# An MoE, attention, MoE kernel on one core: the first expert loop waits per expert for its split weights, and eleven of the sixteen low halves are split inside its tiles

## The reference

```python
def ffn(x, W_gate, b_gate, W_e, b_e):          # 8 experts of 512 x 512
    logits = x @ W_gate + b_gate
    _, top_idx = jax.lax.top_k(logits, 2)
    y_all = relu(einsum('bsd,edh->bseh', x, W_e) + b_e)
    return take_along_axis(y_all, top_idx[..., None], axis=2).mean(axis=2)

x = x + 0.5 * ffn(layernorm(x))
x = x + attention(layernorm(x))                # one head of width 128
x = x + 0.5 * ffn(layernorm(x))
```

## Time and profile before

| | us |
|---|---|
| runs | 308.06, 308.17, 309.02 |
| median | 308.17 |
| the profiled execution, own time | 310.12 |
| its span, first to last instruction | 308.4 |

### The profile page before, as it was taken

One profiled execution on the slowest core, in us unless ns is written; L12 is line 12 of the kernel. 1 busy time (PEld: TensorE's weight loads), 2 busy tenths in 40 slices (PEclk: granted clock), 3 DMA queues, 4 the chain that ended last, 5 costly groups with the idle time before them and its releaser, 6 DMA issues. The chain is left out here.

```text
span 308.4 us, 4811 instructions
## 1 busy us (share of the span) xinstructions
PE 250.2 (81%) x1271; PEld 183.7 (60%) x1272; DVE 182.6 (59%) x387; ACT 98.5 (32%) x177; POOL 148.7 (48%) x152
## 2 busy tenths in 40 slices
PE   6828717799999999976999996639999999999500
PEld 2404403488888888844878774314888888888300
DVE  3999999534444443477778657783344344443691
ACT  0654805123323324211324534211223323324100
POOL 4482682636566565324954500005366566563450
PEclk9575755999999999997999998956999999999955
DMA  7996820584444434624130111103354434345892
GB/s 251 382 403 206 315 83 0 145 272 161 145 162 143 131 130 160 198 68 141 67 136 2 68 70 57 56 26 102 104 167 156 150 129 152 123 159 201 268 344 94
DMA packets 22434, 47.24 MB, mean 153 GB/s; under 512 B 4237, under 2 KB 4877, under 8 KB 22417
## 3 DMA queue, kind: packets, MB, share of 16 engines
q0 software_dynamic: 7360, 20.46, 20.6%
q1 hardware_dynamic: 12208, 22.35, 20.5%
q10 hardware_dynamic: 2850, 4.23, 3.7%
HBM read 32.34 MB, written 18.35 MB: 164 GB/s over the span
## 5 line engine op out<-in xcount | busy, mean ns | idle before, releaser
L447 POOL DMA_INDIRECT z_dram<-yrow,place x46 | 46.8, 1017 | 59.8 <-ACT yrow L574 50.3
L1100 DVE TENSOR_TENSOR xt_lo<-tp_ps,xt_hi 128x512 fp32r<-128x512 f32 x46 | 31.8, 692 | 57.6 <-ACT xt_hi L567 56.4
L439 POOL DMA_INDIRECT xg<-xn_dram,tok x46 | 46.4, 1009 | 33.7 <-DVE tok L1087 18.7
L574 ACT ACTIVATE yrow<-ypre 128x512 f32<-128x512 f32 x46 | 29.1, 632 | 100.7 <-DVE ypre L1108 62.1
L567 ACT ACTIVATE xt_hi<-tp_ps 128x512 fp32r<-128x512 f32 x46 | 26.8, 582 | 11.8 <-PE tp_ps L748 11.8
L748 PE MATMUL tp_ps<-ident,xg 128*128 128x128 f32 x184 | 28.2, 277 | 2.0 <-DMA xg<-xn_dram,tok 1.6
L432 POOL TENSOR_TENSOR rstd<-var_eps,neg_half 128x2 f32<-128x2 f32 x12 | 9.4, 786 | 42.1 <-DVE var_eps L953 39.9
L1108 DVE TENSOR_TENSOR ypre<-y_ps,be_bc 128x512 f32<-128x512 f32 x24 | 16.6, 692 | 21.8 <-PE y_ps L763 21.8
L748 PEld LDWEIGHTS tp_ps<-ident,xg 128*128 128x128 f32 x184 | 22.9, 141 | 10.1 <-DMA xg<-xn_dram,tok 2.6
L763 PE MATMUL y_ps<-whi,xt_hi 128*128 x96 | 28.1, 415 | 0.7 <-issue 0.7
L763 PE MATMUL y_ps<-whi,xt_lo 128*128 x96 | 26.3, 396 | 0.0
(11 more groups left out here) (138 smaller groups left out, 395.7 us busy)
## 6 DMA issues: line engine op xcount, KB each, us to landing
raw<-in_L_ffn_W_e_dram SPq DMA_DIRECT2D x16, 512.0 KB, 6.3
z_rows<-z_dram SPq DMA_DIRECT2D x8, 512.0 KB, 3.8
xn_dram<-xn ACTq DMA_DIRECT2D x12, 256.0 KB, 2.2
x<-in_L_attn_x_dram SPq DMA_DIRECT2D x4, 512.0 KB, 5.7
z_last<-z_dram SPq DMA_DIRECT2D x4, 512.0 KB, 5.9
out_dram<-x SPq DMA_DIRECT2D x8, 256.0 KB, 3.7
xn_dram<-xn_more ACTq DMA_DIRECT2D x4, 256.0 KB, 2.7
z_rows<-z_dram SPq DMA_DIRECT2D x4, 256.0 KB, 2.8
```

Of the source, the lines that this page charges most:

```text
L439: pool.indirect_dma_start(out=xg[:, t % XG, :], out_offset=None, in_=xn_dram[f][:, :], in_offset=bass.IndirectOffsetOnAxis(ap=tok[:, t:t + ...
L447: pool.indirect_dma_start(out=z_dram[f][:, :], out_offset=bass.IndirectOffsetOnAxis(ap=place[:, t:t + 1], axis=0), in_=yrow[:, t % YB, :], ...
L574: act.activation(yrow[:, t % YB, :], ypre[:, t % 2, :], ACT.Relu, scale=HALF_MEAN).then_inc(yrow_made, 1)
L1100: dve.tensor_tensor(xt_lo[:, t % 2, :], tp_ps[(n0 + t) % 2][:], xt_hi[:, t % 2, :].bitcast(F32), ALU.subtract).then_inc(xt_made, 1)
```

## The change

It touches the program up to the end of tile 7 of the first expert loop.

- **Waits.** TensorE no longer waits for all weights ahead of the loop. Product t (t < 8) of the first loop waits until 2(t + 1) high and as many low halves are made. The list gives each expert at least one tile (`thresh` is -1 for the first count), so tile t never belongs to an expert above t. The first eight tiles are therefore written out (`HEADS`), and two rounds of six and three single tiles follow.
- **Splits.** GpSimd makes no low halves. VectorE makes 0 and 1 between the batches, 2 to 4 after the list, and 5 to 15 inside tiles 0 to 6 (2, 2, 2, 2, 1, 1, 1), between `lo_rows(t + 1)` and `bias(t)`. ScalarE makes high halves 0 to 10 ahead of the loop (one per batch from the second batch on, the rest around the mark) and 11 to 15 in tiles 0 to 4, behind `relu(t)`.
- **x and its norm.** x is loaded by tiles. ScalarE normalises, as Identity with scale rstd and bias `off` = -mean * rstd; VectorE computes `off` per batch, one batch behind its moments.
- **Biases.** Two loads on SP's queue broadcast them to all partitions (4 experts each, half of `be_bc`). VectorE waits for the first at tile 0 and for the second at tile 4. The matmuls and copies for them are gone.
- **SP's queue.** x by tiles, halves 0 to 7, the eight stores of xn (until now on ScalarE's queue, each waits for its tile), the first bias load, halves 8 to 15, the second bias load. `raw` has room for all, so `AHEAD` is gone.
- **Warm-ups.** 12 instead of 6 at the start, 3 ahead of the first gate, 2 after each gate, 4 and 12 around the last count; 10 instead of 14 after the list; the 6 ahead of the loop are gone.

```diff
-        WARM = [14, 10]
-        WARM_SPLIT = 6
+        WARM = [10, 10]
...
-        DVE_HALVES = [1, 3, 5, 7, 12, 13, 14, 15]
-        POOL_HALVES = [n for n in range(2 * E) if n not in DVE_HALVES]
-        BE_ACT = [E - 2, E - 1]
+        HI_AHEAD = 11
+        LO_AHEAD = 5
+        LO_IN_TILE = [2, 2, 2, 2, 1, 1, 1]
...
-        HEAD, STEP = 2, 6
+        HEADS, STEP = (E, 2), 6
...
@@ sync
+            for i in range(NT):
+                sp.dma_start(x[:, i, :], x_rows[i * P:(i + 1) * P, :]).then_inc(x_in_sem[i], 16)
+            for n in range(E):
+                load_half(n)
+            for i in range(NT):
+                sp.wait_ge(xn_made, i + 1)
+                sp.dma_start(xn_dram[0][i * P:(i + 1) * P, :], xn_at(i)).then_inc(xn_stored[i], 16)
+            load_be(0)
+            for n in range(E, 2 * E):
+                load_half(n)
+            load_be(1)
...
@@ gpsimd
-            for n in POOL_HALVES:
-                split_lo(pool, n, lo_made_pool)
...
@@ scalar
+            def normalise(i):
+                act.wait_ge(off_made, i // TB + 1)
+                act.activation(xn_at(i), x[:, i, :], ACT.Identity, bias=off[:, i:i + 1],
+                               scale=rstd[:, i:i + 1]).then_inc(xn_made, 1)
...
+                hi_left = list(range(HI_AHEAD, 2 * E)) if f == 0 else []
                 hi_rows(0, n0 + 1, None)
-                for t in range(HEAD + STEP):
+                for t in range(head + first * STEP):
                     tile(t)
+                    if hi_left:
+                        split_hi(hi_left.pop(0))
...
@@ tensor
+                    if f == 0 and t < E:
+                        pe.wait_ge(hi_made, 2 * (t + 1))
+                        pe.wait_ge(lo_made, 2 * (t + 1))
...
-                if f == 0:
-                    warm_up(WARM_SPLIT)
-
-                    pe.wait_ge(lo_made_dve, len(DVE_HALVES))
-                    pe.wait_ge(lo_made_pool, len(POOL_HALVES))
-                    pe.wait_ge(be_copied, E - len(BE_ACT))
-                    pe.wait_ge(be_copied_act, len(BE_ACT))
...
                 gate(0, b)
+                warm_up(2, sp_ps)
...
+            warm_up(4, sp_ps)
             count(0, B - 1)
-            broadcast_be(biases.pop(0))
+            warm_up(12, sp_ps)
             token_list(0)
...
@@ vector
                 def tile(t):
                     if t + 1 < NS:
                         lo_rows(t + 1, n0 + t + 2)
+                    if f == 0 and t < len(LO_IN_TILE):
+                        for _ in range(LO_IN_TILE[t]):
+                            split_lo(dve, halves.pop(0), lo_made)
                     bias(t, t, f * NS + t + 1, f * NS + t - 1 if f or t >= 2 else None)
```

More of the change, by code:

```diff
@@ L324, in _, with load_half @@
         def _(sp):
[L325 to L331, removed]
+            def load_half(n):
                 rows = w_e[n // 2].rearrange("(c p) h -> p c h", p=P)
@@ L612, in softmax @@
                                    accum_out=psumrow[:, q:q + 1]).then_inc(prob_made, 1)
+            his = list(range(HI_AHEAD))
+            for i in range(TB):
+                normalise(i)
             act.wait_ge(gate_in, 32)
             for b in range(B):
+                for i in range(TB * (b + 1), min(TB * (b + 2), NT)):
+                    normalise(i)
                 if b:
@@ L618, in _ @@
                 copy_gate(0, b)
[L619 to L620 removed]
+                if b:
+                    split_hi(his.pop(0))
             copy_logits(0, B - 1)
[L622 removed]
+            while len(his) > 3:
+                split_hi(his.pop(0))
+            mark_partition(0)
+            for n in his:
                 split_hi(n)
[L624 to L630 removed]
             experts(0)
@@ L797, in experts @@
                                 r * STEP + (f * NS + t - 1))
-                for t in range(REST, NS):
+                for t in range(REST[f], NS):
                     tile(t)
@@ L858, in _ @@
             pe.wait_ge(const_made, PE_CONSTS)
-            warm_up(6)
-            pe.wait_ge(be_in, 16)
-            biases = list(range(E))
-            for _ in range(2):
-                broadcast_be(biases.pop(0))
+            warm_up(12)
             for b in range(B):
@@ L1089, in route @@
                     tile_experts(f)
-                for n in halves_left:
-                    split_lo(dve, n, lo_made_dve)
-                count_sent(f)
+                if f:
+                    count_sent(f)
             def experts(f):
@@ L1109, in bias @@
                                       be_bc[:, bass.ds(e * H, H)], ALU.add).then_inc(ypre_made, 1)
+                halves = list(range(LO_AHEAD, 2 * E)) if f == 0 else []
                 def tile(t):
@@ L1158, in add_bv @@
                                   ).then_inc(v_made, 1)
-            biases = [e for e in range(E) if e not in BE_ACT]
             for b in range(B):
-                dve.wait_ge(x_in_sem[b], 16)
                 moments("g0", b)
                 if b:
-                    normalise("g0", b - 1)
-            normalise("g0", B - 1)
-            for _ in range(2):
-                copy_be(biases.pop(0))
+                    offsets(b - 1)
+            offsets(B - 1)
             dve.wait_ge(const_made, CONSTS)
-            todo = list(DVE_HALVES)
-            split_lo(dve, todo.pop(0), lo_made_dve)
-            for b in range(B):
-                copy_be(biases.pop(0))
-                if b:
-                    split_rank(0, b - 1)
-                choose(0, b)
-                if b + 1 < B:
-                    split_lo(dve, todo.pop(0), lo_made_dve)
-                if b:
-                    row_hots(0, b - 1)
-            route(0, todo)
+            choose(0, 0)
+            split_lo(dve, 0, lo_made)
+            choose(0, 1)
+            split_rank(0, 0)
+            row_hots(0, 0)
+            split_lo(dve, 1, lo_made)
+            choose(0, 2)
+            split_rank(0, 1)
+            row_hots(0, 1)
+            choose(0, 3)
+            split_rank(0, 2)
+            row_hots(0, 2)
+            route(0)
+            for n in range(2, LO_AHEAD):
+                split_lo(dve, n, lo_made)
             experts(0)
```

113 lines of the change are left out of this document (53 added, 60 removed).

## The result

| | before | after |
|---|---|---|
| runs | 308.06 to 309.25, 4 | 304.61 to 306.40, 4 |
| median, us | 308.60 | 304.94 |
| the profiled execution, own time | 310.12 | 304.77 |
| its span | 308.4 | 303.0 |

The ratio of after to before is 0.9881 [0.9851, 0.9912]: faster by 1.2%. I had forecast 304.0 (298 to 309). The profiled execution of before lay 1.5 us above its median and that of after did not, so the two traces differ by more (5.4 us) than the medians (3.7). A run over 1.5% above the fastest of its kernel counts as slow and is left out; that was so for one run of all, in `best5`.

The account below looks back on a forecast made before the run. The prediction took VectorE, slowed by GpSimd's splits, to bound the lead-in, with gathers holding product 0. A gain of 15.4 us there less 11.2 lost in the loop gave -4.2: 304.0 us against the median, range 298 to 309.

Parts of the forecast that it names:

- What bounds the kernel: Lead-in before product 0: VectorE bounds it, ten instructions losing 11.9 us beside GpSimd; gathers, not the weight wait, hold product 0.
- The list: End of the lead-in: token list ready at 35.5 us (33.8 to 39.9), against 52.01 before.
- a round of ScalarE: Lead-in, per batch: two normalisations, logits, two gate copies and a split on ScalarE take 4.0 us.
- my slower round: Lead-in, per batch: TensorE at the lower clock takes 5.0 us, putting the last gate copy at 27.6.
- From the list to product 0: First gathers and transposes: 7.9 us with three splits beside them, plus 1.1 for traffic; product 0 at 44.5.
- The traffic term: First gathers: loads on SP's queue until about 40 us delay them by 1.1 us (0 to 4.2).
- The ring: First loop's early tiles: VectorE and ScalarE steps wait on each other in a circle, 5.75 us a tile against 3.24; 10.7 lost.
- 0.5 for the clock: First loop: 0.5 us added because TensorE, idle some 2 us in each slowed tile, may lose clock.
- The sum: Whole kernel: 15.4 us gained in the lead-in, 11.2 lost in the loop, -4.2; 304.0 against the median.
- A: First loop: splits hide behind VectorE's and ScalarE's room, only four tiles losing 0.5 us each; 294.8, chance 0.08.
- B: First loop, tiles 3 to 6: TensorE at the lower clock, 6.5 us a tile, 15.1 lost; 307.9 to 311.2, chance 0.14.
- C: First gathers: transfers delay them 4.2 us, product 0 at 47.6; 307.1, or 309 and more with late weights; chance 0.12.

Follow-up runs that it names:

- best5: Changed kernel with bias(t) ahead of the lo splits, nine lo halves ahead of the loop, 30 warm-ups behind the list, late loads spread over several tiles: 295.88 us, 0.9554.
- wait_only: The kernel before with only the waits per expert and the eight tiles written out, all else as it was: 308.67 us, 0.9996 of before.
- gpsimd_beside: The changed kernel plus six 128x1024 subtractions on GpSimd that feed nothing, in the lead-in: 307.94 us, 0.9962 of before.
- loads_late: The changed kernel with raw halves 11 to 15 and the second bias load issued behind the third gather's landing: 300.54 us, 0.9745 of before.
- no_warm: The changed kernel without TensorE's warm-ups between the batches and around the last count: 304.49 us, 0.9856 of before.
- bias_first: The changed kernel with bias(t) moved ahead of the lo splits of tile t on VectorE: 297.20 us, 0.9620 of before.

## Why the prediction was right

- **What bounds the kernel.** Right: the wait for all weights held nothing (`wait_only`), GpSimd stretched VectorE (`gpsimd_beside`, 5.9 us on five instructions; for ten, my rows gave 11.9), and the gathers stood before product 0.
- **The list, 31.2 against 35.5 (33.8 to 39.9).** The one number outside its bounds, on the good side. The first gate copies ended at 11.6 (12.6). My terms for a round of ScalarE add up to 4.0 us, but I summed three rounds of 3.8. In these I had also counted a normalising pair and a split too many: two pairs were left (the third batch's and the fourth's), and the last split stands behind the last copy, where I counted it again. The three rounds took 9.7 together, though a normalisation cost 0.81 on ScalarE, not 0.63, and the last copy ended at 21.3 instead of 24. From there to the list 9.9 us passed, against 9.8 by my working without the warm-ups' delay. The 1.7 us that I had added for that delay and TensorE's lower clock did not come: PEclk was 1.00 from 6 to 34 us. So my slower round, TensorE's, was never put to the test; at the full clock TensorE held the last copy by 0.69 us.
- **From the list to product 0, 11.5 against 9.0.** The traffic term was mis-sized: 3.7 us, not 1.1, still inside its bound of 4.2. I had set the end of the queue (37 us of transfers, so 40) against the gathers' issue and taken little, since "most of the queue is gone". What counted is whether transfers are still full when the gathers fly, and they were: 406 GB/s from 40 to 41 us, 16 from 43 to 44. `loads_late` shows all 3.7.
- **The ring, 5.68 against 5.75 us a tile.** Right in every link: 4.64 with one split (4.6), 3.61 without a high half (3.6). Product 7 came 34.5 after product 0 against 33.4; the rest is product 0 at the lower clock (2.07 us for its first four matmuls instead of 1.18), which delays product 1 by 1.1. I had 0.5 for the clock.
- **The sum.** -17.1 + 11.8 = -5.3 for the profiled execution (-5.35 measured), against -15.4 + 11.2 = -4.2. The list came 4.3 us sooner than forecast, the gathers cost 2.5 more and the loop 0.6 more, which leaves 1.1: that the sum came out so close is in part luck. The medians differ by 3.7, less than the traces, since the profiled execution of before was above its median; that 304.0 lies 0.9 below the measured 304.94 owes something to both.
- **Rivals.** A is out: the splits do not hide. B: the clock did fall in the ring, but from 62 to 66 us alone, around product 4, and not in every tile from 3 to 6 as it said; the ring hid it. Windows of after:

```profile
54.00:60.00 6.00, 3.45 (x16) 2.69 (x16) 3.56 (x4) 2.38 (x5) 3.02 (x2) 1.00 0.30 100
60.00:66.00 6.00, 4.62 (x14) 3.58 (x15) 3.56 (x4) 2.38 (x4) 3.02 (x2) 0.72 0.28 91
```

  PEclk is 1.00 in one and 0.72 in the other; TensorE is busier, and VectorE, ScalarE and GpSimd do the same work in both, at 5.68 us a turn. The Trainium skill (TensorE: Matmul & The Clock Gate, HAM oscillation — how this bites in real kernels) describes the fall; this trace shows it too, but not its price in time, since TensorE was not the bound. C: of its 4.2 us 3.7 came, and the faster list paid for them.

## What to carry over

When work is moved into a loop that has room by busy time, follow the chain through the orders of all its engines: a step that stands between two others on a ring costs its full length each turn, and one call moved past it gave back 8 us. So did the plainest edit, keeping all splits ahead of the loop; it is worth a run before work is spread over the tiles. A wait that looks like the bound may free nothing; ask which transfer releases the next instruction, and what else is in flight then. Here the transfers moved out of the way of one gather met the next.

## What I had not expected of the hardware

- A gather's issue on GpSimd took 0.94 to 0.98 us alone and 1.74 to 2.02 us beside VectorE's 128x1024 splits, but only if it began while a split ran. In the changed kernel's loop the issue at 50.58, 0.06 us behind the start of two splits, took 2.00; the one at 67.62, 0.02 us ahead of a split, took 0.97; the one at 76.81, with 0.23 us of a split left, 1.07.
- Beside GpSimd's subtractions (2.35 us each) small instructions of VectorE suffered as large ones did: a 128x4 cast took 1.43 us instead of 0.17, while neighbours of the same size kept their time.
- Lower clock on TensorE twice cost nothing: 0.50 to 0.77 ahead of the list in `no_warm`, 0.72 in the ring. It did cost time where TensorE was the bound: 1.1 us in product 0 of the changed kernel, 1.6 behind the wait of product 7 in `bias_first`.
